# Two chunks of a recurrence divided by one reciprocal of their product, in a three-stage decoder layer

## The reference

```
x = layernorm(x + attention(x))            # 16 heads of 32, causal softmax
x = layernorm(x + wkv(x, ctx))             # recurrence over the 256 tokens of a batch
x = layernorm(x + moe_attention(x))        # one key and value head picked for each token

def step(carry, kv_t):                     # wkv, for each channel by itself
    aa, bb, pp = carry
    kt, vt = kv_t
    ww = u + kt
    q = maximum(pp, ww)
    e1, e2 = exp(pp - q), exp(ww - q)
    y_t = (e1 * aa + e2 * vt) / (e1 * bb + e2)
    ww2 = pp + w
    q2 = maximum(ww2, kt)
    e1b, e2b = exp(ww2 - q2), exp(kt - q2)
    return (e1b * aa + e2b * vt, e1b * bb + e2b, q2), y_t
```

## Time and profile before

| | |
|---|---|
| time, three runs | 1698.02 us median (1695.05 to 1698.56) |
| profiled execution | 1698.18 us, its span 1696.3 us |
| mean granted TensorE clock | 0.969 of full speed |
| PE matmuls busy | 1441.8 us, 85% |
| DVE busy | 1098.0 us, 65% |
| ACT busy | 647.6 us, 38% |
| POOL busy | 412.2 us, 24% |

### The profile page before, as it was taken

One profiled execution on the slowest core, in us unless ns is written; L12 is line 12 of the kernel. 1 busy time (PEld: TensorE's weight loads), 2 busy tenths in 40 slices (PEclk: granted clock), 3 DMA queues, 4 the chain that ended last, 5 costly groups with the idle time before them and its releaser, 6 DMA issues.

```text
span 1696.3 us, 29719 instructions
## 1 busy us (share of the span) xinstructions
PE 1441.8 (85%) x9792; PEld 1132.0 (67%) x9792; DVE 1098.0 (65%) x2258; ACT 647.6 (38%) x1459; POOL 412.2 (24%) x552
## 2 busy tenths in 40 slices
PE   6779889898988989898898889989898898989755
PEld 5667767666776766677676667766676776667443
DVE  4475756758576675857667575666857667585644
ACT  3442433425243342524335243442524334252312
POOL 1351312304032131412304131230413223040210
PEclk8879999999999999999999999999999999999779
DMA  6332321323223132321313232132322213232010
GB/s 178 122 82 70 72 64 48 87 56 90 66 61 79 44 89 58 84 72 43 96 30 93 69 72 72 38 89 55 94 69 66 69 47 87 56 90 55 14 50 14
DMA packets 63090, 118.24 MB, mean 70 GB/s; under 512 B 14288, under 2 KB 32720, under 8 KB 63056
## 3 DMA queue, kind: packets, MB, share of 16 engines
q1 hardware_dynamic: 60944, 113.60, 26.6%
q10 hardware_dynamic: 2112, 4.19, 0.7%
HBM read 32.81 MB, written 8.39 MB: 24 GB/s over the span
## 4 chain that ended last, share of the span: by engine, by line
PE 54%; DVE 25%; issue 8%; ACT 7%; DMA 3%; POOL 1%; SPq 1%; DVEq 1%; ACTq 0%; POOLq 0%
PE pp L443 11%; PE pp L445 10%; PE pp L444 10%; PE po L541 5%; DVE neg_max L1282 4%; PE sq L489 2%; DVE w_key L1357 2%; DMA q_stack<-max_rows 2%; PE po L545 2%; DVE w_max L1352 2%; DVE w_val L1448 2%; PE po L555 2%; DVE o_tok L1307 2%; DVE stats L1313 2%; PE sq L468 2%
## 5 line engine op out<-in xcount | busy, mean ns | idle before, releaser
L957 ACT ACTIVATE prob<-sk 128x512 f32<-128x512 f32 x384 | 215.2, 594 | 444.2 <-PE sk L468 443.9
L1282 DVE TENSOR_REDUCE neg_max<-sq 128x2 f32<-128x512 f32 (+1 forms) x384 | 249.8, 678 | 42.0 <-PE sq L468 34.2
L443 PE MATMUL pp<-xt_hi,w_hi 128*128 128x256 f32 x736 | 222.3, 302 | 13.8 <-DVE w_lo L1269 7.1
L444 PE MATMUL pp<-xt_lo,w_hi 128*128 128x256 f32 x736 | 209.6, 285 | 0.0
L445 PE MATMUL pp<-xt_hi,w_lo 128*128 128x256 f32 x736 | 209.5, 285 | 0.0
L443 PE MATMUL pp<-w_hi,xt_hi 128*128 128x512 f32 x380 | 164.7, 433 | 24.1 <-DVE w_val L1448 21.9
L443 PEld LDWEIGHTS pp<-xt_hi,w_hi 128*128 128x128 f32 x736 | 142.3, 193 | 21.9 <-issue 11.8
L445 PE MATMUL pp<-w_hi,xt_lo 128*128 128x512 f32 x380 | 154.0, 405 | 0.0
L444 PE MATMUL pp<-w_lo,xt_hi 128*128 128x512 f32 x380 | 153.9, 405 | 0.0
L444 PEld LDWEIGHTS pp<-xt_lo,w_hi 128*128 128x128 f32 x736 | 142.5, 194 | 0.7
L445 PEld LDWEIGHTS pp<-xt_hi,w_lo 128*128 128x128 f32 x736 | 142.3, 193 | 0.0
(11 more groups left out here) (183 smaller groups left out, 3317.2 us busy)
## 6 DMA issues: line engine op xcount, KB each, us to landing
q_stack<-q_hi SPq DMA_DIRECT2D x256, 128.0 KB, 2.3
q_stack<-q_lo SPq DMA_DIRECT2D x128, 128.0 KB, 2.3
k_stack<-k_hi SPq DMA_DIRECT2D x128, 128.0 KB, 2.3
x_raw<-in_xT SPq DMA_DIRECT2D x16, 512.0 KB, 3.6
k_stack<-k_lo SPq DMA_DIRECT2D x64, 128.0 KB, 2.3
xa<-in_x SPq DMA_DIRECT2D x16, 512.0 KB, 3.5
w_val<-in_ctxT SPq DMA_DIRECT2D x64, 128.0 KB, 2.1
out_y<-xb SPq DMA_DIRECT2D x16, 512.0 KB, 2.8
```

Of the source, the lines that this page charges most:

```text
L443: T.matmul(out, lh, rh, start=(c == 0), stop=False, skip_group_check=True)
L444: T.matmul(out, lh, rl, start=False, stop=False, skip_group_check=True)
L957: A.activation(dst, sk[n % 2][:], ACT.Exp, scale=SCALE).then_inc(s_exp, 1)
L1282: V.tensor_reduce(dst, src, AX.X, ALU.max, negate=True).then_inc(s_max, 1)
```

## The change

One reciprocal serves the two chunks of a pair. GpSimd multiplies the two denominators into `w_y[:, 1]`, and VectorE takes the reciprocal r of that product in place. Meanwhile GpSimd multiplies each numerator by the other chunk's denominator, in place in `w_ev`. Then each quotient is its crossed numerator times r: n0 d1 / (d0 d1) and n1 d0 / (d0 d1). The second quotient overwrites r. The cap on the present key's exponent is 30 instead of 60.

A batch so has two divides instead of four, and ten multiplications and quotients on GpSimd instead of four. The places in the orders move too, as the diff shows.

```
-NOW_HIGH = 60.0
+NOW_HIGH = 30.0
...
-            def divide(b, c):
-                dve.wait_ge(w_den, 2 * (CC * b + c) + 1)
-                V.reciprocal(w_key[:, c % HC, :], w_key[:, c % HC, :]).then_inc(w_rec, 1)
+            def divide(b, pair):
+                dve.wait_ge(w_both, HC * b + pair + 1)
+                both = w_y[:, 1, :]
+                V.reciprocal(both, both).then_inc(w_rec, 1)
...
@@ VectorE, iteration: the divide behind maxima_a(t, 1), of the batch before @@
-                    divide(b, 3)
+                    divide(b, 1)
@@ VectorE, iteration: divide(t, 0) stays ahead of recurrence_start(t, 2) @@
                     recurrence_start(t, 3)
-                    divide(t, 1)
...
-                if do_a:
-                    divide(t, 2)
...
@@ VectorE, opening @@
                 qk_lo(1, PA_K)
+                qk_lo(1, PA_K + 1)
                 divide(0, 0)
-                qk_lo(1, PA_K + 1)
-                divide(0, 1)
                 recurrence_start(0, 3)
...
                 sums(0, 3)
-                divide(0, 2)
                 second_residual(0, 0)
...
-            def quotient(b, c):
-                i = c % HC
-                pool.wait_ge(w_den, 2 * (CC * b + c + 1))
-                pool.wait_ge(w_rec, CC * b + c + 1)
-
-                wait(pool, w_job, W_JOBS * (b - 1) + W_YJ + 2 if c < HC else W_JOBS * b + W_YJ + 1)
-                G.tensor_tensor(w_y[:, i, :], w_ev[:, i, :], w_key[:, i, :], ALU.mult).then_inc(w_yr, 1)
+            def cross(b, pair):
+                c = HC * pair
+                pool.wait_ge(w_den, 2 * (CC * b + c + HC))
+                wait(pool, w_job, W_JOBS * b + W_YJ + 1 if pair else W_JOBS * (b - 1) + W_YJ + 2)
+                G.tensor_tensor(w_y[:, 1, :], w_key[:, 0, :], w_key[:, 1, :], ALU.mult).then_inc(w_both, 1)
+                for i in range(HC):
+                    G.tensor_tensor(w_ev[:, i, :], w_ev[:, i, :], w_key[:, 1 - i, :], ALU.mult).then_inc(w_cross, 1)
+
+            def quotients(b, pair):
+                pool.wait_ge(w_cross, CC * b + HC * (pair + 1))
+                pool.wait_ge(w_rec, HC * b + pair + 1)
+                for i in range(HC):
+                    G.tensor_tensor(w_y[:, i, :], w_ev[:, i, :], w_y[:, 1, :], ALU.mult).then_inc(w_yr, 1)
...
@@ GpSimd, iteration @@
                 products(t, 0)
                 products(t, 1)
-                quotient(t, 0)
+                cross(t, 0)
+                quotients(t, 0)
                 weighted(t, 2)
-                quotient(t, 1)
                 weighted(t, 3)
                 products(t, 2)
                 products(t, 3)
+                cross(t, 1)
                 if prev:
                     inverse_std(t - 1, 2)
                     third_bias(t - 1)
-                quotient(t, 2)
-                quotient(t, 3)
+                quotients(t, 1)
                 ones_back(t)
```

More of the change, by code:

```diff
@@ L208, in build @@
         w_carry, w_first, w_now, w_evr, w_scan = sem("w_carry"), sem("w_first"), sem("w_now"), sem("w_evr"), sem("w_scan")
-        w_den, w_rec, w_yr, w_ones = sem("w_den"), sem("w_rec"), sem("w_yr"), sem("w_ones")
+        w_den, w_rec, w_yr, w_ones, w_both, w_cross = sem("w_den"), sem("w_rec"), sem("w_yr"), sem("w_ones"), sem("w_both"), sem("w_cross")
         ln_stat = [sem(f"ln_stat{n}") for n in range(3)]
```

## The result

The changed kernel takes 1714.14 us (1713.83 to 1715.2, four runs), the kernel before 1697.07 us beside it (1695.05 to 1698.56, four runs). The ratio is 1.0102, with a 95% interval of 1.0085 to 1.012: 1.0% slower. The prediction had 1706.5 us, slower, in a range of 1690 to 1720. The profiled execution's span is 1712.5 us, 16.2 more than before.

What follows compares the result with a forecast made beforehand. TensorE carried 54% and VectorE 25% of the chain, with TensorE waiting for VectorE before the score maxima. Profiled time, fourteen iterations, opening, last batch and clock: 1698.2 + 9.8 + 1.3 + 0.8 - 3.6 = 1706.5 us; range 1690 to 1720.

Steps and rivals of the forecast that it cites:

- Third norm: GpSimd's three multiplications ahead of its power and bias delay ScalarE 2.65 us; `max_rows` +1.3, head's scores +0.7 per iteration.
- First pair: VectorE's reciprocal ends 1.9 us later, `k_lo` +1.4, TensorE's values +0.8, scores at 813.4 instead of 812.52.
- Second pair: Most of TensorE's 1.66 us idle at the maxima goes, but VectorE's saving is used up at the y transpose: +0.1 us.
- Crosses: GpSimd's multiplications in the second pair, beside maxima reading PSUM, take 0.73 us each, not 1.20 as beside scans.
- Opening: Chunk 2's context product comes behind both quotients of the first pair, making the maxima 1.3 us late: +1.3 us.
- Last batch: Nothing covers its second pair; GpSimd's last quotients end at 1619.45 instead of 1618.65: +0.8 us.
- the clock: Six slow iterations cost 1.2 us each, 7.2 together; with the idle at the maxima mostly gone, half comes back: -3.6 us.
- likeliest case: The forecast itself: the third norm's delay reaches the head's scores, 14 x 0.7 us; 1706.5 us, range 1698 to 1713, chance 0.36.
- the rival in which the clock falls more often: New idle stretches of TensorE take the clock in 12 iterations instead of six: 1717 us; chance 0.12.
- a number of slow iterations other than three: Listed sign of being wrong: a count other than three of iterations slowed by a granted clock below 1.00.
- hidden third norm: ScalarE gets its bias at most 2.0 us later, TensorE doesn't wait at the head's scores: say 1691 us; chance 0.24.
- Company on GpSimd: Products or crosses meet scans or additions to `xb`; 0.5 us more per iteration reaches the third norm: 1717 us; chance 0.10.

Runs made afterwards that it cites:

- e7: Kernel before with only the first pair sharing a reciprocal, ahead of the start of chunk 2; second pair as before: 1721.44 us, ratio 1.0104.
- e3: e2 with GpSimd's third-norm power and bias put between product and crosses: 1685.31 us, ratio 0.9924 to the kernel before.
- e2: Changed kernel with the first pair's two reciprocals and quotients back at their old places, only the second pair sharing: 1693.97 us, ratio 0.9971 to the kernel before.
- e1: Changed kernel with GpSimd's third-norm power and bias back ahead of the second pair's product and crosses: 1708.49 us, ratio 1.0064 to the kernel before.
- e5: Changed kernel with the start of chunk 2's recurrence moved ahead of the first shared reciprocal on VectorE: 1694.72 us, ratio 0.9964 to the kernel before.
- e6: e5 with the third norm's GpSimd work put between the second pair's product and crosses: 1684.31 us, ratio 0.9898 to the kernel before.
- e4: Kernel before with three more unused multiplications on GpSimd between chunk 3's products and the third norm: 1703.72 us, ratio 1.0035.
- e8: Kernel before with five more unused multiplications on GpSimd ahead of the third norm: 1720.57 us, ratio 1.0119.
- e10: Kernel before with only the present key's cap changed from 60 to 30: 1699.9 us, ratio 0.9985.
- e11: The same kernel as e6, timed again beside the kernel before: 1686.93 us, ratio 0.9916.
- e9: e6 with the second pair's shared reciprocal ahead of the head's third score maximum instead of behind it: 1685.26 us, ratio 0.9905 to the kernel before.

## Why the prediction was right, point by point

*The side and the mechanism.* Slower, with no VectorE time kept at the y transpose and a delay through the third norm. Three effects add up in an undisturbed iteration. Stall of the first pair: +0.7 (e7). Saving of the second pair: -0.6 (e3). Third norm: +0.7 (e2 less e3) or +0.5 (changed kernel less e1). Sum: 0.6 to 0.8; measured 0.8 (100.5 or 100.6 against 99.8). The prediction had 0.7.

The four kernels in which both pairs share say the same:

| undisturbed iteration, us | third norm behind the crosses | third norm ahead of them |
|---|---|---|
| reciprocal ahead of the start of chunk 2 | 100.5 (changed kernel) | 100.0 (e1) |
| start of chunk 2 first | 99.6 (e5) | 99.1 (e6) |

The stall costs 0.9 us in either column, the third norm's delay 0.5 in either row, and without both the iteration is 0.7 shorter than before. In e7, where the second pair is as before, the stall costs 0.7; what makes the difference of 0.2 was not tried.

*First pair.* Predicted: reciprocal 1.9 us later, `k_lo` +1.4, values +0.8, scores at 813.4. Measured: 2.0, 1.4, 0.8, 813.4. That the lateness travels on through the maxima and SyncE's queue was right.

*Second pair.* Predicted: the 1.66 us idle mostly gone, y transpose +0.1. Measured: 0.38 left, +0.2. The maxima were put at 815.35 and start at 815.7, after 0.27 us of waiting for TensorE.

*Third norm.* Predicted: ScalarE +2.65, `max_rows` +1.3, scores +0.7 (823.6 less 822.97 is 0.63, rounded up). Measured: +2.65, +1.1, +0.86, with 0.60 us of idle. The point at which the delay begins to count was put at 2.0 us of third-norm delay; e4 shows about 2.1 (ScalarE's wait grew from 0.32 to 2.64 us, and the scores waited for the last 0.22 of it).

*Crosses.* Taken at 0.73 each because they run beside maxima from PSUM; the two of the second pair took 1.42 together. The Trainium skill, "SBUF — State Buffer", section "Who interferes with whom", has a VectorE instruction with at most one SBUF input, outside the two-port modes, not contend with GpSimd, and the trace agrees with these 1.42 us.

*Opening.* +1.3 predicted, +1.2 measured at the first `x2` transpose.

*Last batch.* +0.8 predicted. Its second pair falls in the fifteenth iteration, which takes 96.2 us instead of 96.1, and what follows the last landmark is 0.4 shorter. So nothing of it can be seen in the whole.

**The step that was mis-sized is the clock**: "idle of 1.7 us before 803.9, 1.5 before the y transpose and 0.6 before 823.6 comes. I take half back: -3.6." The idle at 803.9 came, and in six iterations the clock fell at it instead. Among the fourteen iterations eight are slow instead of six. Over their undisturbed neighbours they are longer by 11.7 us in sum (102.2, 102.2, 101.9, 101.7, 102.3, 102.3, 101.8 and 101.7, against 100.55), where the six of before gave 7.9. So the clock cost 3.8 us and gave nothing back: 7.4 off, nearly the whole distance of the sum (+8.3) to the measured +16.2. The rest is 0.1 us more in each iteration and about 1 us less at the two ends. Without the clock the prediction's terms give +11.9 us, and the traces 16.2 - 3.8 = +12.4.

These counts come from one trace on each side, and the clock differs between executions of one kernel. The kernel before ran 45 times beside the experiments, from 1691.76 us at a mean granted clock of 0.975 to 1709.51 at 0.961. The fourteen of these with a clock of 0.964 to 0.966, which is what the changed kernel's four executions had, took 1698.5 to 1704.3 us, 1701.9 in the mean; the changed kernel's took 1714.3. That is 12.4 us apart at the same clock, as the traces have it, and the rest of the 17 us, about 4.6, is the clock's.

So part of the hit is luck. The likeliest case's own range ended at 1713, below the measured 1714.14, and the time lies nearer to the 1717 of the rival in which the clock falls more often than to 1706.5. By its last paragraph the prediction also called a number of slow iterations other than three a sign of being wrong; there were eight. Its lower end is off too: 14 x 0.2 + 1.3 + 0.8 - 7.2 gives 1696, not 1698.

The rivals: hidden third norm is refuted by the changed kernel's wait for `max_rows` and by e1, e2 and e8. Company on GpSimd is refuted by the durations, since every product, cross and quotient of the iteration shown took 0.72 or 0.73 us. The rival of more frequent falls of the clock (chance 0.12) is the part of the truth that the forecast lacked, though its twelve slow iterations were not reached by any trace; e7 has ten with a fall. That the clock's falls hang on these idle stretches is shown by e2, e3, e5 and e6, in which TensorE's idle at the maxima and at `o_tok` is both shorter than 1 us or gone: none, none, one and one of fourteen iterations are slow, and the slow one of e5 and e6 is the first, with a fall just behind TensorE's wait of 2.0 us for `xb`.

## What to carry to other kernels

When two reciprocals are merged, the merged one must wait for the later operand: look at what stands behind it in its engine's order, and put something there that doesn't need it. Here the 1.1 us start of the next chunk, put there, made the difference between +1.0% and -0.4%, part of it through the clock.

Work that goes to an idle engine delays everything behind it in that engine's order, across several queues; count the slack of each (2 us here) before counting the engine's share of the span. What the other chain needs first (the product, then the third norm) goes first, and what has time (the crosses) last.

## What the runs showed of the hardware

A short idle of TensorE can cost more than itself. Idle of 1.7 to 1.9 us at the maxima, in a stretch otherwise well filled, was followed by 3.4 us or more at half the clock in six of 14 iterations of the kernel before, in six of e10, which has the same instructions, and in seven of e4. Idle of 1.6 us at `o_tok` was followed by it in six of the changed kernel and six of e1. With both kinds of idle, e7 has it in ten. With neither, e2, e3 and e11 have no such fall and e9 has one, just behind the first landmark; the longest of their recurring waits in these stretches is 1.2 us, at the y transpose. That isn't a sharp bound: e5 has one fall behind a wait of 0.98 us. Removing one idle place while opening another moved the falls, it didn't end them.

A fall costs 1.3 us an iteration in the kernel before and 1.1 to 1.8 in the changed one. Where TensorE would wait for something else soon after, it costs less or nothing: in e5 the iteration from 529.0 to 628.6 has a mean clock of 0.98 and takes 99.6 us like its neighbours, while its wait for `max_rows` is 0.18 us instead of 0.61; and e8 shows the same in most of its ten. Which of several like iterations is hit stays open; nothing was tried on it.
